# Medians searched with one count to a filter round instead of two, and finished beside the convolutions

## The chip, the core and the metric

The kernel runs on one core of one Trainium2 chip. Its engines work on their own instruction queues and meet at semaphores: TensorE multiplies matrices (PE in the profile), VectorE (DVE), ScalarE (ACT) and GpSimd (POOL) do the rest, and SyncE (SP) issues the DMAs. The metric is the device time of one launch in microseconds.

## The reference, cut to what matters

Two layers run on 16 images of 64 channels of 128x128. The first adds, for each image and channel, the negative part of the channel's median, and filters up and down with a ReLU between; the second gates the spectrum of the image, and lets its pixels attend to 320 keys and values that two strided convolutions make.

```python
q_in = jnp.quantile(x.reshape(B, C, -1), 0.5, axis=-1)
x = x + jax.nn.relu(-q_in)[:, :, None, None]
y = upfirdn2d(x, lpf, up=2, padding=6, gain=4.0)
y = upfirdn2d(jnp.maximum(y, 0.0), lpf, down=2)
spec = jnp.fft.rfft2(y, norm='ortho'); mag = jnp.abs(spec)
gate = sigmoid(w2 @ gelu(w1 @ mag))
xf = y + jnp.fft.irfft2(spec * gate, s=(128, 128), norm='ortho')
# q = xf @ q_w; k, v from conv(xf, stride 8) and conv(xf, stride 16), layer norm, projections
out = proj(softmax(q @ k.T / 4) @ v) + y
```

The median of 16384 numbers is the mean of the 8192nd and the 8193rd.

## The kernel before, in words

The program first takes the median of the first image with nothing beside it (`first_vector`, `first_scalar`, `first_gpsimd`, `first_tensor`), and then loops 16 times over a body that computes one image and, beside it, the median of the next. A channel lies on two partitions (p and p + 64) with 8192 numbers on each, in `xc`.

The median is written as one generator for each engine (`pe_median`, `act_median`, `pool_median`, `dve_median`, lines 188 to 358). A `yield` ends a piece, and the body calls `slot(n)` at fixed places to put the next n pieces into the engine's queue there. The order of work is so written out by hand; an engine that reaches a piece whose semaphore isn't up yet stands still with all that is behind it.

The pieces before are, in this order:
- 8 of the range: VectorE takes the maximum and the minimum of each quarter (line 273); TensorE swaps the halves; VectorE halves the range 26 times (line 290) and makes the first middle (292).
- 78 of the search, 26 steps of 3 counts. In each VectorE counts the numbers up to the middle in one part (line 300) and ScalarE in the other with a sign (line 236). After three pieces TensorE sums the partitions (lines 201 and 202), VectorE adds the six counts and makes the next middle (307, 310, 312), and GpSimd and VectorE keep the lowest upper bound (252, 254, 304). Both engines wait for the middle before they count on. This is called a step's turnover below.
- 8 of the last count: VectorE counts the numbers up to the bound found (line 318), and TensorE sums (208).
- 17 of the next larger number: for each eighth of `xc` VectorE makes a mask (330), GpSimd adds the numbers (261), and VectorE takes the minimum (335).
- a closing chain of small steps between TensorE and VectorE (lines 214 to 224 and 338 to 358), whose last copy writes `sB` and raises `md_end`.

The body of an image goes through these stages:
- The filter, 37 rounds (n) for 32 pairs of channels, in software pipeline: TensorE widens (459), ScalarE copies (1040), TensorE filters across (469), ScalarE applies the ReLU (1046), TensorE narrows (480), VectorE copies (818), TensorE transposes (499), VectorE copies (832), and every other round TensorE narrows the other way (490) and VectorE copies (825). The rest columns go an own way through bank 7. GpSimd adds the rest rows to 16 channels at once (1216). There are 2 slots in a round from n = 2 on, 70 in all.
- The spectrum, 17 rounds with one slot: lines 517 to 535, copies 853 and 857.
- The magnitudes are transposed (546, copies 866), the gate network follows (556, 569, ScalarE's 1085 and 1090), with 9 slots in its middle.
- The inverse, 16 groups (586 to 599, VectorE's 879 and 885), with 16 slots; what is left of the median comes behind it.
- The turn: 16 groups of 4 transposes (618), which VectorE (895) and ScalarE (1109) copy by turns. No slots. The fourth group waits for `md_end`.
- The convolutions: the first with 32 taps (649), the second with 128 in four parts (638), and between them four pieces of the queries (TensorE 630, ScalarE 1117, VectorE 903, GpSimd 1245 and 1247), and VectorE's addition of the bias to `Z` (911).
- A small chain makes keys and values; meanwhile SyncE lays out the queries with 24 DMAs for a unit (`load_unit`, line 382), two units in a row, and then the maxima (1304). The queries lie over `xc`.
- Attention, 32 tiles.

## Time and profile before

| | |
|---|---|
| median of 3 runs | 12,843.6 us (12,840.56 to 12,852.78) |
| the profiled execution | 12,841.47 us, of it a span of 12,840.0 us |
| TensorE, VectorE, ScalarE, GpSimd busy | 84%, 73%, 57%, 20% |
| mean granted TensorE clock | 0.904 |
| first median, alone | from 18.3 us to 260.9 us |
| one image | 784 us, 16 times |

Times in a profile are microseconds from the span's start. A row of groups says line, engine, operation, what is written and read with shapes, how often; then busy us, the mean ns of one, and the us that the engine stood idle before them, with what ended that. In a row of the timeline the first two numbers are the start and the us that it took; a bracket holds the idle time before. Busy time of TensorE is modelled and overlaps between matmuls. The image looked at below is the sixth; it begins at 4210.1 us.

### The profile page before, as it was taken

How to read it: one execution, taken by the hardware profiler on the slowest of the kernel's cores; microseconds unless marked ns; L12 is line 12 of the kernel's file. 1: busy time of each engine (PE TensorE's matmuls, PEld its weight loads, DVE VectorE, ACT ScalarE, POOL GpSimd, SP SyncE). 2: the span in 40 equal slices, each digit the busy share in tenths (PEclk: the TensorE clock that was granted, in tenths of full speed). 3: DMA queues.
4: the chain of work that ended last, by engine and by line, in shares of the span. 5: the costliest groups of instructions: out<-in, count | busy, mean ns of one | idle time of the engine just before them, and what ended most of it. 6: DMA issues, size and time to landing. Idle time of an engine off the chain costs nothing. (4 is left out here: it accounts for less than half of the span.)

```text
span 12840.0 us, 193091 instructions
## 1 busy us (share of the span) xinstructions
PE 10730.5 (84%) x70049; PEld 5483.5 (43%) x70049; DVE 9433.9 (73%) x16044; ACT 7283.6 (57%) x12109; POOL 2610.8 (20%) x4040
## 2 busy tenths in 40 slices
PE   1797888978879798897988889788897887979889
PEld 1543535334353443534435354353534435344353
DVE  7867667776777767768777686767777677776776
ACT  4656455564646646466464565646566464664646
POOL 1211202112131221302212021121211213122130
PEclk9898898988989899898998989889898898989989
DMA  1021120211202022120211202112021221202212
GB/s 45 18 43 42 39 61 18 50 35 43 57 26 55 21 49 52 28 67 7 54 47 34 66 13 46 43 40 60 18 53 31 45 56 27 53 21 49 52 28 66
DMA packets 169035, 532.27 MB, mean 41 GB/s; under 512 B 64008, under 2 KB 86536, under 8 KB 153168
## 3 DMA queue, kind: packets, MB, share of 16 engines
q1 hardware_dynamic: 168016, 519.00, 17.2%
q8 instruction: 601, 9.85, 0.3%
q14 instruction: 418, 3.42, 0.1%
HBM read 230.38 MB, written 67.11 MB: 23 GB/s over the span
## 5 line engine op out<-in xcount | busy, mean ns | idle before, releaser
L949 DVE TENSOR_REDUCE R<-ps 128x2 f32<-128x640 f32 x4096 | 3195.4, 818 | 941.5 <-PE ps L687 930.6
L1157 ACT ACTIVATE R<-ps 128x512 f32<-128x512 f32 x5120 | 2823.2, 594 | 671.5 <-PE ps L708 645.3
L236 ACT ACTIVATE R<-R,st 128x1475 bf16<-128x1475 f32 x1326 | 2022.9, 1526 | 862.5 <-DVE st L312 687.6
L300 DVE TENSOR_SCALAR_CACHE_REDUCE R<-R,st 128x1255 bf16<-128x1255 f32 x1326 | 2012.0, 1517 | 21.3
L687 PE MATMUL ps<-KST,R 96*128 96x320 bf16 x8192 | 1888.4, 314 | 60.7 <-DVE R L949 50.5
L733 PE MATMUL ps<-R 128*32 128x512 f32 x12288 | 1648.8, 609 | 38.0 <-DVE Wk L903 32.9
L708 PE MATMUL ps<-R,KST 104*128 104x512 bf16 x4096 | 1583.7, 389 | 21.4 <-ACT R L1157 20.6
L687 PEld LDWEIGHTS ps<-KST,R 96*128 96x128 bf16 x8192 | 764.8, 100 | 828.6 <-DVE R L949 313.0
L1245 POOL CAST R<-Wk 128x512 bf16<-128x512 f32 x256 | 283.8, 1109 | 2980.4 <-DVE Wk L903 2980.4
L201 PE MATMUL ps<-st,cst 128*128 128x3 f32 x884 | 176.0, 269 | 697.7 <-DVE R L300 464.4
L480 PE MATMUL ps<-R,cst 128*64 128x512 f32 x2048 | 648.5, 715 | 109.0 <-DVE R L818 109.0
L708 PEld LDWEIGHTS ps<-R,KST 104*128 104x128 bf16 x4096 | 397.8, 98 | 724.8 <-ACT R L1157 457.2
L469 PE MATMUL ps<-R,cst 64*128 64x512 f32 x2048 | 627.4, 692 | 12.7 <-ACT R L1046 12.4
L372 POOL TENSOR_TENSOR R<-R,sB 128x1024 f32<-128x1024 f32 x136 | 255.1, 1897 | 1653.2 <-DMA R<-xh_in 1648.2
L1040 ACT ACTIVATE R<-ps 128x532 f32<-128x532 f32 x512 | 308.0, 601 | 494.0 <-PE ps L459 493.8
L1046 ACT ACTIVATE R<-ps 128x1024 f32<-128x1024 f32 x512 | 521.2, 1018 | 89.9 <-PE ps L469 89.0
L201 PEld LDWEIGHTS ps<-st,cst 128*128 128x128 f32 x884 | 156.5, 215 | 877.7 <-DVE R L300 792.9
L261 POOL TENSOR_TENSOR R<-R 128x1024 f32<-128x1024 f32 x136 | 327.6, 2415 | 963.1 <-DVE R L330 963.1
L1099 ACT ACTIVATE Wk<-ps 128x512 f32<-128x512 f32 x256 | 152.9, 597 | 647.2 <-PE ps L589 647.2
L1152 ACT ACTIVATE Wk<-ps 128x512 f32<-128x512 f32 x512 | 305.7, 597 | 368.7 <-PE ps L733 368.7
L1164 ACT ACTIVATE Wk<-ps 128x256 f32<-128x256 f32 x512 | 196.7, 384 | 554.1 <-PE ps L751 554.1
L879 DVE TENSOR_TENSOR Wk<-R 128x520 f32<-128x520 f32 x256 | 298.1, 1170 | 266.0 <-ACT R L1090 215.5
(208 smaller groups left out, 19968.1 us busy)
## 6 DMA issues: line engine op xcount, KB each, us to landing
R<-R SPq DMA_DIRECT2D x3072, 64.0 KB, 2.4
R<-xh_in SPq DMA_DIRECT2D x136, 512.0 KB, 4.5
out_dram<-Z SPq DMA_DIRECT2D x16, 4096.0 KB, 14.3
R<-xa_in SPq DMA_DIRECT2D x36, 1024.0 KB, 11.4
R<-xb_in SPq DMA_DIRECT2D x34, 1024.0 KB, 12.4
R<-sr_in SPq DMA_DIRECT2D x32, 1024.0 KB, 5.4
R<-sr_in SPq DMA_DIRECT2D x16, 2016.0 KB, 9.2
R<-sr_in SPq DMA_DIRECT2D x16, 1056.0 KB
```

What stands on the lines that cost most here:

```text
L201: e.matmul(P0(NP), lhsT=c("pair"), rhs=cnt[:, 0:NP], start=True, stop=False)
L236: e.activation(junka[:, 0:o2 - o1], xc[:, o1:o2], ACT.Sign, bias=mid, scale=-1.0, accum_out=cnt[:, NP + i:NP + i + 1]).then_inc(md_ca, 1)
L261: e.tensor_tensor(t, t, xs, ALU.add).then_inc(md_tb, 1)
L300: e.tensor_scalar(junk[:, 0:o1 - o0], xc[:, o0:o1], mid, None, ALU.is_le, ALU.add, accum_out=cnt[:, i:i + 1]).then_inc(md_cv, 1)
L469: op = e.matmul(ps[:, 2 + j, :].rearrange("p (c h n) -> p c h n", c=2, h=2), lhsT=ut[r, 133 * j:133 * j + 128], rhs=T1[m % 2][r].rearrange ...
L480: op = e.matmul(ps[64 * j:64 * j + 64, 4, :], lhsT=c(f"d{j}"), rhs=Y[m % 2][:, j, :], start=True, stop=True)
L687: op = e.matmul(ps[:, 2 + 2 * bq + r, 0:320], lhsT=q, rhs=KST[0:96, h0 + r, :], start=True, stop=True)
L708: op = e.matmul(ps[:, g2, :], lhsT=KST[:, h, c0:c0 + 128], rhs=QS[u % 3][:, h, 512 * s4:512 * s4 + 512], start=True, stop=True)
L733: op = e.matmul(ps[32 * h:32 * h + 32, 7, :], lhsT=VX[:, 4 * i + h, :], rhs=PB[:, k, src, :], start=i == 0, stop=i == 2)
L949: e.tensor_reduce(MX[(4 * u + s4) % 2][:, blk_, h0:h0 + 2], ps[:, 2 + 2 * bq:4 + 2 * bq, 0:320], axis=AX.X, op=ALU.max).then_inc(mx, 1)
L1046: e.activation(Y[m % 2], ps[:, 2:4, :], ACT.Relu, scale=4.0).then_inc(yr, 1)
L1157: e.activation(PB[:, t % 2, w, :], ps[:, w % 2, :], ACT.Exp).then_inc(ex, 1)
```

## The change

- The range is the largest magnitude: 4 pieces instead of 8, each one maximum of absolute values, and the search starts at 0. The 26 halvings are one multiplication with a row of constants.
- The last count goes. The 16 masks of the next larger number (512 numbers each now, 16 bit, 0 or 2 to the 100th) are multiplied on TensorE with a pair matrix and summed in a bank, and the count is read from the sum. There are 33 pieces for this instead of 8 and 17.
- The two sums of counts on TensorE take 6 and 3 columns.
- The slots: in the filter one in a round and a second in every fourth, 47 in all instead of 70; 17 in the spectrum as before; 18 instead of 9 from the transposes of the magnitudes to the end of the gate network; none in the inverse; 16 in the turn; 16 in the convolutions, 4 behind the first and 4 behind each of three parts of the second. The rest of the median, the closing chain too, comes behind the last part.
- In a filter round ScalarE's piece stands ahead of the ReLU (1046 before) instead of behind it.
- GpSimd's addition of the rest rows is cut in four, one in each of four rounds (the last block: four in a row).
- SyncE waits for the end of the search before it loads the last taps, and for `md_end` before the queries are laid out.

```diff
-            for i in range(8):
-                yield
-            e.wait_ge(md_cv, NP * STEPS + 8)
-            b7.free(e)
-            e.matmul(P0(8), lhsT=c("pair"), rhs=cnt[:, 0:8], start=True, stop=True).then_inc(md_p, 1)
-            b7.ask()
-            for i in range(17):
-                yield
+            for i in range(17):
+                if i < 16:
+                    e.wait_ge(md_ta, i + 1)
+                    b7.free(e)
+                    for q in range(4):
+                        j = q % 2
+                        op = e.matmul(ps[64 * j:64 * j + 64, 7, 336:464], lhsT=pairb[:, :], rhs=MF[i % 2][:, 128 * q:128 * q + 128],
+                                      start=i == 0 and q < 2, stop=i == 15 and q > 1)
+                    op.then_inc(md_fs, 1)
+                yield
+                if i > 0:
+                    yield
+            b7.reader = (md_r, 1)
+            b7.free(e)
+            e.matmul(P0(1), lhsT=c("pair"), rhs=cnt[:, 0:1], start=True, stop=True).then_inc(md_p, 1)
...
         def pool_median(e):
...
-                    e.tensor_tensor(t, t, xs, ALU.add).then_inc(md_tb, 1)
+                    if i > 1:
+                        e.wait_ge(md_mm, i - 1)
+                    e.tensor_tensor(TF[i % 2], MF[i % 2], xc[:, 512 * i:512 * i + 512], ALU.add).then_inc(md_tb, 1)
...
         def dve_median(e, halves):
...
+                e.tensor_reduce(m1[:, k:k + 1], xc[:, 2048 * k:2048 * k + 2048], axis=AX.X, op=ALU.max,
+                                apply_absolute_value=True).then_inc(md_got, 1)
+                yield
...
-            for k in range(STEPS):
-                e.wait_ge(md_got, 2 + k)
-                e.tensor_scalar(hs[:, k + 1:k + 2], hs[:, k:k + 1], 0.5, None, ALU.mult).then_inc(md_got, 1)
...
+            e.tensor_scalar(hs, c("halves"), hi, None, ALU.mult).then_inc(md_v, 1)
...
-                e.tensor_scalar(junk[:, 0:1024], xc[:, 1024 * i:1024 * i + 1024], hi, None, ALU.is_le, ALU.add,
-                                accum_out=cnt[:, i:i + 1]).then_inc(md_cv, 1)
...
+            for i in range(17):
+                if i < 16:
                     if i > 1:
-                        e.wait_ge(md_mm, i - 1)
-                    e.tensor_scalar(t, xs, hi, BIG, ALU.is_le, ALU.mult).then_inc(md_ta, 1)
+                        e.wait_ge(md_tb, i - 1)
+                        e.wait_ge(md_fs, i - 1)
+                    e.tensor_scalar(MF[i % 2], xc[:, 512 * i:512 * i + 512], hi, BIG, ALU.is_le, ALU.mult).then_inc(md_ta, 1)
                 yield
                 if i > 0:
                     e.wait_ge(md_tb, i)
+                    e.tensor_reduce(mm[:, i - 1:i], TF[(i - 1) % 2], axis=AX.X, op=ALU.min).then_inc(md_mm, 1)
                     yield
+            e.wait_ge(md_fs, 16)
+            e.tensor_reduce(cnt[:, 0:1], ps[:, 7, 336:464], axis=AX.X, op=ALU.add).then_inc(md_r, 1)
...
# tensor, vector, scalar and gpsimd, in each filter round
-                slot(1 if n > 1 else 0)
+                slot(1 if n >= P or n % 4 == 0 < n else 0)
# tensor, the inverse, and the turn
-                    slot(1)
-            for _ in med:
-                pass
...
-                    op = e.transpose(ps[:, 4 + k, 128 * i:128 * i + 128], XF[:, 2 * v:2 * v + 2, :].rearrange("p w c -> p (w c)"),
+                    op = e.transpose(ps[:, k, 128 * i:128 * i + 128], XF[:, 2 * v:2 * v + 2, :].rearrange("p w c -> p (w c)"),
                                      c("ident"))
                 op.then_inc(xt_ps, 1)
+                slot(1)
...
             op.then_inc(c1_ps, 1)
+            slot(4)
             for j in range(1, 4):
                 stage(0, j, 6)
                 conv2(j - 1)
+                slot(4)
             conv2(3)
+            for _ in med:
+                pass
...
# gpsimd
+                    for q in range(i, i + 1 if b < 3 else 4):
+                        rows = Z[:, 16 * b + 4 * q:16 * b + 4 * q + 4, :]
+                        e.tensor_tensor(rows, rows, ZS[:, 4 * q:4 * q + 4, :], ALU.add).then_inc(zad, 1)
# sync
+            e.wait_ge(md_v, STEPS + 2)
             e.dma_start(TAP2[:, 65:128, :], sr2w[:, 65:128, :]).then_inc(in_w2[2], 16)
+            e.wait_ge(md_end, 1)
             load_unit(e, 0)
```

The slots move instructions on every engine. In VectorE's queue in the filter stood, in the second half of the rounds before (818, 825 and 832 are a round's copies, 300 a count, 307 to 312 and 304 the turnover):

```order
L307 TENSOR_REDUCE st<-ps 128x1
L310 TENSOR_SCALAR st<-st 128x1
L312 SCALAR_TENSOR_TENSOR st<-st 128x1
L300 TENSOR_SCALAR R,st<-R,st 128x1255
L304 TENSOR_TENSOR st<-st 128x1
L818 COPY R<-ps 128x512
L825 COPY Z<-ps 128x512
L832 COPY R<-ps 128x2x256
L300 TENSOR_SCALAR R,st<-R,st 128x1256 x2
```

and there stands now (811, 818 and 825 are the same copies):

```order
L307 TENSOR_REDUCE st<-ps 128x1
L310 TENSOR_SCALAR st<-st 128x1
L312 SCALAR_TENSOR_TENSOR st<-st 128x1
L300 TENSOR_SCALAR R,st<-R,st 128x1255
L811 COPY R<-ps 128x512
L818 COPY Z<-ps 128x512
L825 COPY R<-ps 128x2x256
L798 COPY R<-ps 96x261
L300 TENSOR_SCALAR R,st<-R,st 128x1256
L304 TENSOR_TENSOR st<-st 128x1
```

Between two sets of copies stood two counts, and there stands one; the small operation 304 has moved behind the second count.

In TensorE's queue the turn and the convolutions were, before (618 transposes, 630 queries, 649 and 638 the convolutions):

```order
L618 MATMUL ps<-cst,R 128x128 x64
L630 MATMUL ps<-R,cst 128x512
L649 MATMUL ps<-R 64x256 x32
L630 MATMUL ps<-R,cst 128x512
L638 MATMUL ps<-R 64x64 x32
```

and the beginning of the turn is now (606 transposes, 203 and 204 the sums of the last search step, 212 the masks' matmuls):

```order
L606 MATMUL ps<-cst,R 128x128 x4
L203 MATMUL ps<-st,cst 128x6
L204 MATMUL ps<-st,cst 128x3
L212 MATMUL ps<-Wk,pairb 64x128 x4
L606 MATMUL ps<-cst,R 128x128 x4
L212 MATMUL ps<-Wk,pairb 64x128 x4
L606 MATMUL ps<-cst,R 128x128 x8
```

and from the turn's last groups into the convolutions (619, 638 and 627 the queries and the convolutions):

```order
L606 MATMUL ps<-cst,R 128x128 x8
L212 MATMUL ps<-Wk,pairb 64x128 x4
L619 MATMUL ps<-R,cst 128x512
L638 MATMUL ps<-R 64x256 x32
L212 MATMUL ps<-Wk,pairb 64x128 x8
L619 MATMUL ps<-R,cst 128x512
L627 MATMUL ps<-R 64x64 x32
```

Every second group of transposes has four matmuls of a mask behind it, which wait for VectorE.

In VectorE's queue the turn was eight copies (895), then queries (903) and bias (911):

```order
L358 COPY sB<-ps 128x64
L895 COPY R<-ps 128x512 x8
L903 SCALAR_TENSOR_TENSOR Wk<-ps,cst,R 128x512
L911 TENSOR_TENSOR Z<-Z,cst 128x64x32
L903 SCALAR_TENSOR_TENSOR Wk<-ps,cst,R 128x512
```

and it is now, from the first copy (885) on (321 a mask, 325 a minimum):

```order
L885 COPY R<-ps 128x512
L307 TENSOR_REDUCE st<-ps 128x1
L314 TENSOR_TENSOR st<-st 128x1
L321 TENSOR_SCALAR Wk<-R,st 128x512 x2
L885 COPY R<-ps 128x512
L325 TENSOR_REDUCE st<-Wk 128x1
L321 TENSOR_SCALAR Wk<-R,st 128x512
```

A minimum and a mask stand behind each copy, and in the convolutions two of each stand behind each piece of the queries and bias.

## Rows read from the trace of the kernel before

**Rows 1.** Busy us by stretch, sixth image, with granted clock and DMA.
```profile
core 0: us, PE busy (x) PEld busy (x) DVE busy (x) ACT busy (x) POOL busy (x), PEclk, DMA share, GB/s
4210.00:4420.00 210.00, 163.10 (x866) 78.29 (x865) 181.83 (x329) 145.06 (x196) 37.69 (x115) 0.85 0.06 13
4482.00:4515.00 33.00, 22.70 (x119) 17.60 (x119) 16.32 (x28) 13.36 (x15) 5.10 (x2) 0.66 0.00 1
4515.00:4570.00 55.00, 50.68 (x553) 35.56 (x554) 46.96 (x56) 9.55 (x16) 14.18 (x6) 0.95 0.24 91
4570.00:4612.00 42.00, 40.90 (x391) 27.27 (x388) 17.97 (x18) 9.10 (x14) 15.11 (x8) 1.00 0.04 12
4612.00:4645.00 33.00, 20.27 (x66) 7.00 (x66) 21.19 (x35) 3.46 (x8) 18.81 (x30) 0.56 0.53 93
```

**Rows 2.** Timeline of ScalarE, filter rounds of the sixth image: start us, us.
```profile
4249.11 0.59 ACT L1040 ACTIVATE R<-ps 128x532 f32<-128x532 f32 x1
...
4392.56 0.61 ACT L1040 ACTIVATE R<-ps 128x532 f32<-128x532 f32 x1 [0.19 <-PE ps L459]
```

**Rows 3.** Groups by line, of the page.
```profile
L236 ACT ACTIVATE R<-R,st 128x1475 bf16<-128x1475 f32 x1326 | 2022.9, 1526 | 862.5 <-DVE st L312 687.6
L300 DVE TENSOR_SCALAR_CACHE_REDUCE R<-R,st 128x1255 bf16<-128x1255 f32 x1326 | 2012.0, 1517 | 21.3
```

**Rows 4.** Groups by line and shape, whole span.
```profile
L818 DVE COPY R<-ps 128x512 f32<-128x512 f32 x512 | 351.3, 686 | 72.6 <-PE ps L480 71.9
L273 DVE TENSOR_REDUCE st<-R 128x1 f32<-128x2048 f32 x136 | 305.2, 2277 | 8.9 <-DMA R<-xa_in 7.8 <-DMA R<-xb_in 1.1
L895 DVE COPY R<-ps 128x512 f32<-128x512 f32 x128 | 88.6, 692 | 27.8 <-PE ps L618 27.8
```

**Rows 5.** Timeline of ScalarE in the first median, which nothing else runs beside.
```profile
51.98 1.53 ACT L236 ACTIVATE R<-R,st 128x1475 bf16<-128x1475 f32 x1 [1.82 <-DVE st L312]
...
58.72 1.53 ACT L236 ACTIVATE R<-R,st 128x1475 bf16<-128x1475 f32 x1 [1.82 <-DVE st L312]
```

**Rows 6.** Timeline of VectorE in the spectrum, sixth image.
```profile
4445.28 0.69 DVE L853 COPY Wk<-ps 128x512 f32<-128x512 f32 x1
...
4447.76 0.69 DVE L853 COPY Wk<-ps 128x512 f32<-128x512 f32 x1
...
4451.33 0.69 DVE L853 COPY Wk<-ps 128x512 f32<-128x512 f32 x1
```

**Rows 7.** Timeline of VectorE, start of the search, sixth image.
```profile
4240.84 4.87 DVE L290 TENSOR_SCALAR st<-st 128x1 f32<-128x1 f32 x26
```

**Rows 8.** Timeline of the end of the first median, nothing beside it.
```profile
220.73 1.28 DVE L318 TENSOR_SCALAR_CACHE_REDUCE R<-R,st 128x1024 bf16<-128x1024 f32 x1
...
232.24 1.41 DVE L330 TENSOR_SCALAR R<-R,st 128x1024 f32<-128x1024 f32 x2
...
239.85 1.80 DVE L330 TENSOR_SCALAR R<-R,st 128x1024 f32<-128x1024 f32 x1
241.58 1.21 DVE L335 TENSOR_REDUCE st<-R 128x1 f32<-128x1024 f32 x1
241.74 2.34 POOL L261 TENSOR_TENSOR R<-R 128x1024 f32<-128x1024 f32 x1 [0.63 <-DVE R L330]
...
257.47 0.37 PE L214 MATMUL ps<-cst,st 128*1 128x128 f32 x1 [25.54 <-DVE st L338]
...
260.69 0.23 DVE L358 COPY sB<-ps 128x64 f32<-128x64 f32 x1 [0.78 <-PE ps L224]
```

**Rows 9.** Timeline of VectorE beside the addition of line 1216.
```profile
4422.29 3.09 DVE L304 TENSOR_TENSOR st<-st 128x1 f32<-128x1 f32 x1
```

**Rows 10.** Timeline of VectorE in the convolutions, sixth image.
```profile
4595.34 0.75 DVE L903 SCALAR_TENSOR_TENSOR Wk<-ps,cst,R 128x512 f32<-128x512 f32 x1 [12.96 <-ACT R L1117]
...
4600.05 0.75 DVE L903 SCALAR_TENSOR_TENSOR Wk<-ps,cst,R 128x512 f32<-128x512 f32 x1 [1.76 <-ACT R L1117]
```

**Rows 11.** Timeline of SyncE's queue at the start of attention, sixth image.
```profile
4609.51 30.59 SPq L382 DMA_DIRECT2D R<-R  x48
```

More of the change, by code:

```diff
@@ L188, in pe_median @@
         def pe_median(e, b7):
-            for _ in range(8):
+            for _ in range(4):
                 yield
@@ L192, in pe_median @@
             b7.free(e)
-            e.matmul(P0(2), lhsT=c("swap"), rhs=pm, start=True, stop=True).then_inc(md_p, 1)
+            e.matmul(P0(1), lhsT=c("swap"), rhs=pm[:, 0:1], start=True, stop=True).then_inc(md_p, 1)
             b7.ask()
             for k in range(STEPS):
-                for i in range(NP):
+                for _ in range(NP):
                     yield
@@ L226, in act_median @@
         def act_median(e):
-            for _ in range(8):
+            for _ in range(4):
                 yield
@@ L246, in pool_median @@
                 mid = mids[:, k % 2:k % 2 + 1]
-                for i in range(NP):
+                for _ in range(NP):
                     yield
@@ L548, in tensor @@
                 op.then_inc(mt_ps, 1)
+                slot(1 if grp % 3 else 0)
             for grp in range(9):
@@ L559, in tensor @@
                     op.then_inc(h_ps, 1)
-                slot(1)
+                slot(1 if grp % 3 else 0)
             for grp in range(9):
@@ L573, in tensor @@
                 op.then_inc(g_ps, 1)
+                slot(1 if grp % 3 else 0)
             for n in range(18):
@@ L839, in vector @@
                     e.tensor_copy(VM, ps[0:80, 7, 0:128]).then_inc(mq, 1)
-                slot(1 if n > 1 else 0)
+                slot(1 if n >= P or n % 4 == 0 < n else 0)
             for i in range(2):
@@ L866, in vector @@
                 e.tensor_copy(MAGT[:, 512 * grp:512 * grp + 128 * np_], ps[:, 5 + grp % 2, 0:128 * np_]).then_inc(mgt, 1)
-            for grp in range(9):
+                slot(1 if grp % 3 else 0)
+            for grp in range(12):
                 slot(1)
@@ L911, in vector @@
                 e.tensor_tensor(zj, zj, c("pb").unsqueeze(2).to_broadcast([128, C, 32]), ALU.add).then_inc(zb, 1)
+                slot(4)
+            for _ in med:
+                pass
             e.wait_ge(xt_ps, 16)
@@ L1040, in scalar @@
                     e.activation(T1[n % 2].rearrange("p h c n -> p h (c n)"), ps[:, 0:2, 0:266], ACT.Copy).then_inc(t1, 1)
+                slot(1 if n > 1 else 0)
                 m = n - 1
@@ L1046, in scalar @@
                     e.activation(Y[m % 2], ps[:, 2:4, :], ACT.Relu, scale=4.0).then_inc(yr, 1)
-                slot(1 if n > 1 else 0)
                 if n >= 8 and n % 8 == 0:
@@ L1085, in scalar @@
                     e.activation(HID[0:rows, o:o + w], ps[0:rows, k, 0:w], ACT.Gelu).then_inc(gelu, 1)
-                slot(1)
+                slot(1 if grp % 3 else 0)
             for grp in range(9):
@@ L1091, in scalar @@
                              ps[:, 2 + grp % 2, 0:128 * np_].rearrange("p (k c) -> p k c", c=C), ACT.Sigmoid).then_inc(sig, 1)
+                slot(1 if grp % 3 else 0)
             for n in range(18):
@@ L1229, in gpsimd @@
                                     ALU.add).then_inc(mag, 1)
-            for grp in range(9):
-                slot(1)
-            for n in range(18):
-                if n >= 2:
-                    slot(1)
-            for _ in med:
-                pass
+            slot(18)
+            slot(16)
             def stage(g, j, bk):
@@ L1250, in gpsimd @@
                 stage(0, j, 6)
+                slot(4)
+            for _ in med:
+                pass
             steps = 0
```

127 lines of the change are left out of this document (48 added, 79 removed).

## The prediction, made before the changed kernel was run

> **What bounds the kernel now.** I first cut one image into its stages by the busy time of each stretch, then looked for what fills a filter round, then for what a search step costs alone. An image takes 784 us, and some 435 of them come before attention's first scores; the change touches only these. In the filter's 210 us VectorE is busy for 182, ScalarE 145, TensorE 163 at a granted clock of 0.85; in the gate network's 33 us all are half idle; in the inverse's 55 us TensorE is busy for 50.7, in the turn and the convolutions' 42 us for 40.9; then come 33 us in which a chain makes keys and values [rows 1]. From the 7th to the 31st round, 24 of them, the filter takes 143.45 us, or 5.98 a round [rows 2]. Its two slots hold two counts of 1.52 us on VectorE and 1.53 on ScalarE [rows 3], and a round's copies are 0.69 each, two and a half of them [rows 4]: 3.04 + 1.7 = 4.8 us of VectorE. The missing 1.2 us are turnovers, two in three rounds. Alone, a step of three counts takes 6.74 us [rows 5], so a turnover costs 6.74 - 3 x 1.65 = 1.8 us on ScalarE (1.65 us is a count with the reading of its sum, by the 1.53 and the start of the next behind it). Where one slot stands in a round, in the spectrum, rounds follow after 2.48 us, and after 3.57 where a turnover falls between [rows 6]: 1.1 us. So in the filter the median is on the path, counts and turnovers both, and taking some away shortens it. Everywhere else it was hidden well or nearly.
>
> **The first median, once.** Its second half waits for data until 28 us, so of the four reductions less only two count: -4.5 us, by 2.277 [rows 4]. The 26 halvings, 4.87 us, become one operation: -4.8 [rows 7]. From the last count's start to the first mask are 11.5 us, which go, and one sum more comes, 0.9. The masks took 232.24 to 257.47, 25.2 us for 8 [rows 8]: a mask waits for GpSimd, then a mask (0.7), and an addition (2.34) follow each other. 16 halves do the same in 16 x (0.4 + 1.2) = 25.6. Together -19.5 us.
>
> **The filter, each image.** Four reductions less: -9.1; the halvings -4.8. The 25 rounds from there on keep 31 of 50 counts and 10.3 of 16.7 turnovers. VectorE: 1.25 x 1.57 + 1.8 for copies = 3.8; turnovers, one in 2.4 rounds, at 1.1 to 1.8, are 0.45 to 0.75; so 4.2 to 4.5. TensorE is busy for 163 / 37 = 4.4 us a round now, at the clock of 0.85 [rows 1], and has to do all of it but a third of the sums. It is so near that neither hides behind the other; I take 4.6, with 4.2 and 5.1 for ends. 25 x (5.98 - 4.6) = -34.5. The last 5 rounds keep their slots. A small operation of VectorE stood 3.09 us behind GpSimd's addition of the rest rows as the spectrum began [rows 9]; of a quarter it could be held a quarter as long: -2. Sum -50 (-60 to -38).
>
> **The spectrum** keeps its 17 slots: 0.
>
> **The gate network.** 18 slots, 6 steps, where 9 were. In the transposes VectorE has 6 x 1.57 + 9 copies (5.8) + two turnovers (1.6) = 17 us. Behind them ScalarE is later: 12 counts of 1.65, of which the last is beside the inverse, 18.1; its own 13.4 [rows 1]; of four turnovers two in full and one in part, 4.4: 36. 53 us against 33: +20 (+16 to +25). This is where counts no longer have a cover.
>
> **The inverse.** TensorE is busy for 50.7 of 55 us; that is what can be won: up to -4.3, taken as -3.5 since VectorE has no masks left there and the closing chain is gone.
>
> **The turn.** Eight copies of VectorE with the idle time before them are (88.6 + 27.8) / 16 = 7.3 us an image [rows 4]. TensorE's queue now holds a mask's matmuls behind every second group. A ring closes: group of transposes (0.45 at full clock, double at half), VectorE's copy 0.69, a minimum (0.6, half of 1.21), a mask (0.4), the matmuls (0.3), handoffs 0.2: 2.6 to 3.1 for two groups, where 0.9 was. Of the last, most is at half clock, for TensorE is idle over half of it, as in the stretch behind the convolutions (0.56 granted, 20.3 of 33 us busy [rows 1]). 7 such, and the search's last turnover with two masks at the start, 4: 23 to 26 us. +17.
>
> **The convolutions.** Four parts with 32 more matmuls. The queries follow each other after 4.71 us [rows 10]; VectorE now has query 0.75, bias 2.3, two minima and two masks, 2.0, behind 0.8 of handoff: 5.9, and TensorE stands before the second mask. Two such rounds cost +1.5 to +3.6 each, the third has one mask to wait for, +1.5; the first convolution starts at half clock, +1.5. +8.
>
> A mask behind GpSimd's work is the open point. Alone, masks of 0.7 us took 1.80 while an addition ran [rows 8]. The Trainium skill (SBUF — State Buffer, Who interferes with whom) says that a tensor_scalar in a two-port mode and a GpSimd instruction block each other for a whole instruction, and a reduction never does. By that rule, and this trace agrees with 1.80 against 0.7, a mask also waits for GpSimd's subtraction of the queries and for the addition of the mask before.
>
> **The closing chain** took 3.45 us, 257.47 to 260.92 [rows 8], and has one sum more, 4.3. It stood in the inverse's end; now keys and values wait for it, and SyncE's queue, which began 2.5 us before the convolutions' end (4609.51 against 4612.0 [rows 1, 11]), begins 4.4 behind it. 24 copies of 0.64 us and a landing come before the first maxima, so +4.3 to +6.9: I take +5.4.
>
> **Sum.** -50 + 20 - 3.5 + 17 + 8 + 5.4 = -3.1 us an image, 16 times -50; with -19.5 the profiled 12,841.5 become 12,772. The median of the runs is 2.1 us more than the profiled execution; I say 12,775 us. Two large terms stand against each other: rounds that get 1.4 us shorter, and places where the same counts and masks have less cover.
>
> **Rivals.**
> - Rounds of 4.2 us. For it: VectorE's sum allows it. Against: TensorE's 4.4. It gives 25 x 0.4 x 16 = 160 less: 12,615.
> - Masks never blocked. The convolutions then cost 3.5 and not 8, the turn 15: 6.5 x 16 = 104 less, 12,670. The page's rule speaks against it; with the rule in force at every mask of the convolutions they cost 10.5: +40, 12,815, at the edge of what can be told from before.
> - Slower: TensorE stands in its own queue before masks, and works at half clock when it goes on. The turn then takes 4 us for two groups, and the first convolution, 15 us at the full clock of 1.00 that [rows 1] show, has half of it at 1.2 GHz. That is +7 and +7.5, 14.5 an image, +232: 13,005. For it: 0.56 of the clock where TensorE is busy 20 of 33 us. Against: the ring's parts add up to 3.1 at most. It decides from where turn and convolutions take over 72 us together (they are 42 now, 67 in my sum).
> - Filter rounds of 5.1: TensorE's busy 4.4 is the bound and the waits of the coupled engines come on top. +12.5 an image, +200: 12,975, slower.
> - The change takes out the counts it says; 25 rounds with 31 counts stand in the code. Only the gain could be missing, which is the rival before.
>
> **How the numbers follow.** My forecast has 0.40, and its own range is 12,700 to 12,830 us; rounds of 4.2 us 0.12; masks never blocked 0.07, blocked everywhere 0.07; the slower rival 0.20; rounds of 5.1 us 0.14. Under 0.2%, some 26 us, a measurement of this kernel can't tell from no change. Faster: 0.38 of the forecast, 0.12, 0.07, 0.01: 0.58. The same: 0.02, and most of blocked everywhere, 0.05, and 0.03 of the two slower cases: 0.10. Slower: 0.32. The range leaves out the outer parts of the first and third rivals: 12,590 to 12,990.
>
> **What would show it.** Right: the filter from first widening to the spectrum in 155 to 172 us, rounds of 4.3 to 5.0; the gate network 49 to 58 us; the turn 20 to 28 us with TensorE waiting for masks; the convolutions with 4.7 stretched to 6 to 8; `md_end` about 4 us behind the last convolution, and keys and values behind it. The masks, 512 numbers, would take 0.4 us free and over 1 us behind GpSimd. Wrong: rounds over 5 us; a gate network under 45 us, which would say that counts hide beside sigmoids; a turn under 15 us; an attention that changes its length.

## The result, and the profile after

The changed kernel takes 12,803.8 us (median, 12,786.4 to 12,843.3), the kernel before in the same session 12,850.9 (12,834.3 to 12,871.4), 20 runs each. The ratio is 0.9967, 95% interval 0.9960 to 0.9974: faster by a third of a per cent. The profiled execution took 12,798.9 us (span 12,797.6), 42.6 less than that of before. I had said 12,775.

A small sum of large terms, as forecast. The medians over the 16 images, in us from an image's first matmul, cut at the first matmul of each stage (the last line is the mean from one image's start to the next, and the line above it what is left of that):

| stage | before | after | change | predicted |
|---|---|---|---|---|
| first median, once | 280.0 | 259.9 | -20.1 | -19.5 |
| filter, with the search's range | 210.0 | 168.8 | -41.2 | -50 |
| spectrum | 62.6 | 56.5 | -6.1 | 0 |
| gate network | 33.3 | 51.2 | +17.9 | +20 |
| inverse | 53.9 | 49.8 | -4.1 | -3.5 |
| turn | 9.0 | 28.1 | +19.1 | +17 |
| convolutions | 33.1 | 39.7 | +6.6 | +8 |
| last convolution to first scores | 33.5 | 39.1 | +5.6 | +5.4 |
| first scores to the next image | 349.5 | 350.5 | +1.0 | 0 |
| an image | 784.9 | 783.7 | -1.2 | -3.1 |

16 times -1.2 and -20.1 are -39; the spans differ by 42.4.

The sixth image by stretch, in the order of the table without the spectrum (turn and convolutions, one row in [rows 1], are two here; columns: us, busy us and instructions of each engine, granted clock, DMA share, GB/s):

```profile
4177.70:4346.20 168.50, 141.41 (x841) 68.81 (x841) 135.04 (x237) 115.90 (x160) 39.80 (x116) 0.94 0.06 13
4402.70:4454.00 51.30, 33.45 (x141) 24.80 (x141) 36.80 (x71) 39.10 (x50) 2.48 (x12) 0.50 0.00 0
4454.00:4504.00 50.00, 49.76 (x544) 35.26 (x544) 24.15 (x32) 10.24 (x18) 0.00 (x0) 0.94 0.18 65
4504.00:4532.00 28.00, 18.21 (x105) 13.87 (x106) 14.47 (x28) 4.78 (x8) 10.51 (x11) 0.63 0.20 74
4532.00:4572.00 40.00, 34.77 (x336) 20.17 (x337) 20.68 (x24) 4.30 (x6) 25.18 (x16) 0.96 0.01 2
4572.00:4611.00 39.00, 24.24 (x93) 9.11 (x89) 23.24 (x48) 3.46 (x8) 17.82 (x27) 0.55 0.50 82
```

The filter's clock rose from 0.85 to 0.94, the gate network's fell to 0.50, where TensorE is busy for 33 of 51 us and waits in between; the inverse is full. The turn, nearly full before, has TensorE busy for 18 of 28 us at 0.63. ScalarE's copy of the widened rows in rounds 7 and 31 of this filter (counted from 0), as in [rows 2]:

```profile
4204.59 0.61 ACT L1034 ACTIVATE R<-ps 128x532 f32<-128x532 f32 x1
4318.35 0.61 ACT L1034 ACTIVATE R<-ps 128x532 f32<-128x532 f32 x1 [0.65 <-PE ps L453]
```

That is 113.76 / 24 = 4.74 us a round, where it was 5.98. Now the turn, two groups of the ring on VectorE, GpSimd and TensorE (timeline: start us, us, engine, line, idle before and its releaser):

```profile
4510.70 0.69 DVE L885 COPY R<-ps 128x512 f32<-128x512 f32 x1 [2.57 <-PE ps L606]
4511.31 0.67 DVE L325 TENSOR_REDUCE st<-Wk 128x1 f32<-128x512 f32 x1
4511.90 0.48 DVE L321 TENSOR_SCALAR Wk<-R,st 128x512 bf16<-128x512 f32 x1
4512.44 0.30 PE L212 MATMUL ps<-Wk,pairb 128*64 128x128 bf16 x4 [1.08 <-DVE Wk L321]
4512.46 1.17 POOL L270 TENSOR_TENSOR Wk<-Wk,R 128x512 f32<-128x512 bf16 x1 [2.19 <-DVE Wk L321]
4512.67 1.09 PE L606 MATMUL ps<-cst,R 128*128 128x128 f32 x8
4513.37 0.69 DVE L885 COPY R<-ps 128x512 f32<-128x512 f32 x1 [0.98 <-PE ps L606]
...
4515.10 0.42 PE L212 MATMUL ps<-Wk,pairb 128*64 128x128 bf16 x4 [1.33 <-DVE Wk L321]
...
4515.45 1.97 PE L606 MATMUL ps<-cst,R 128*128 128x128 f32 x8
4516.60 0.69 DVE L885 COPY R<-ps 128x512 f32<-128x512 f32 x1 [1.56 <-PE ps L606]
```

VectorE waits for TensorE's group (L606), TensorE for VectorE's mask (L321): neither is full. A turn of this ring of waits takes 2.67 us with 8 matmuls at full clock (1.09) and 3.23 at half (1.97). In the convolutions the queries on VectorE, 4.71 us apart in [rows 10], follow each other after 7.40, with two minima (L325) and two masks (L321) between:

```profile
4550.67 0.75 DVE L894 SCALAR_TENSOR_TENSOR Wk<-ps,cst,R 128x512 f32<-128x512 f32 x1 [10.91 <-ACT R L1108]
4551.34 2.28 DVE L902 TENSOR_TENSOR Z<-Z,cst 128x2048 f32<-128x2048 f32 x1
4553.54 0.68 DVE L325 TENSOR_REDUCE st<-Wk 128x1 f32<-128x512 f32 x1
4554.14 0.47 DVE L321 TENSOR_SCALAR Wk<-R,st 128x512 bf16<-128x512 f32 x1
4554.53 0.68 DVE L325 TENSOR_REDUCE st<-Wk 128x1 f32<-128x512 f32 x1
4555.12 0.78 DVE L321 TENSOR_SCALAR Wk<-R,st 128x512 bf16<-128x512 f32 x1
4558.07 0.75 DVE L894 SCALAR_TENSOR_TENSOR Wk<-ps,cst,R 128x512 f32<-128x512 f32 x1 [2.17 <-ACT R L1108]
```

The second mask stands beside GpSimd's subtraction of the query, which ends at 4555.62, and takes 0.78 us where the first took 0.47. Over the whole trace 48 of the 112 masks in the convolutions took 0.8 us, and none of the 144 in the turn.

The median ends 3.9 us behind the last convolution (4573.3), and keys and values begin behind it:

```profile
4577.00 0.22 DVE L352 COPY sB<-ps 128x64 f32<-128x64 f32 x1 [0.78 <-PE ps L234]
4577.25 0.41 DVE L907 MEMSET R<- 64x424 f32 x1
```

### The profile page after: what moved, and what is told of

It is laid out like the page before. It is cut to its first block and busy times, and to the rows that moved or that the text cites. A ratio compares the mean times of both kernels' runs of the same rounds, so it can differ in the third digit from the quotient of the medians.

```text
span 12797.6 us, 195926 instructions
## 1 busy us (share of the span) xinstructions
PE 10782.9 (84%) x71137; PEld 5569.1 (44%) x71137; DVE 8883.3 (69%) x15501; ACT 7238.6 (57%) x12109; POOL 2641.9 (21%) x4368
## 5 line engine op out<-in xcount | busy, mean ns | idle before, releaser
L300 DVE TENSOR_SCALAR_CACHE_REDUCE R<-R,st 128x1255 bf16<-128x1255 f32 x1326 | 2011.3, 1517 | 20.8
L463 PE MATMUL ps<-R,cst 64*128 64x512 f32 x2048 | 569.2, 630 | 102.8 <-ACT R L1041 94.9
L203 PE MATMUL ps<-st,cst 128*128 128x6 f32 x884 | 187.1, 283 | 540.3 <-DVE R L300 217.4
L366 POOL TENSOR_TENSOR R<-R,sB 128x1024 f32<-128x1024 f32 x136 | 254.9, 1895 | 1642.4 <-DMA R<-xh_in 1636.8
L474 PE MATMUL ps<-R,cst 128*64 128x512 f32 x2048 | 562.8, 628 | 21.1 <-ACT R L1041 21.1
L1108 ACT ACTIVATE R<-ps,cst 128x512 bf16<-128x512 f32 x256 | 175.9, 687 | 670.7 <-PE ps L619 670.7
L1041 ACT ACTIVATE R<-ps 128x1024 f32<-128x1024 f32 x512 | 517.6, 1011 | 44.5 <-PE ps L463 44.5
L1143 ACT ACTIVATE Wk<-ps 128x512 f32<-128x512 f32 x512 | 305.7, 597 | 369.2 <-PE ps L726 369.2
L878 DVE TENSOR_TENSOR R<-ps,Z 128x512 f32<-128x512 f32 x256 | 269.7, 1063 | 350.8 <-PE ps L595 350.8
L262 POOL TENSOR_SCALAR st<-st 128x1 f32<-128x1 f32 x442 | 99.5, 225 | 1974.6 <-DVE st L307 1961.1
```

Source lines behind the costliest of these rows:

```text
L203: e.matmul(P0(2 * NP), lhsT=c("pair"), rhs=cnt[:, 0:2 * NP], start=True, stop=False)
L300: e.tensor_scalar(junk[:, 0:o1 - o0], xc[:, o0:o1], mid, None, ALU.is_le, ALU.add, accum_out=cnt[:, i:i + 1]).then_inc(md_cv, 1)
L463: op = e.matmul(ps[:, 2 + j, :].rearrange("p (c h n) -> p c h n", c=2, h=2), lhsT=ut[r, 133 * j:133 * j + 128], rhs=T1[m % 2][r].rearrange ...
L474: op = e.matmul(ps[64 * j:64 * j + 64, 4, :], lhsT=c(f"d{j}"), rhs=Y[m % 2][:, j, :], start=True, stop=True)
L1041: e.activation(Y[m % 2], ps[:, 2:4, :], ACT.Relu, scale=4.0).then_inc(yr, 1)
```

## The experiments

Each kernel ran 4 to 11 times, by turns with the kernel before; the ratio is to that one. "Changed" is 12,804 us, from its own session.

| run | us | ratio, 95% interval | against changed |
|---|---|---|---|
| addition in one piece | 13,096 | 1.0196 (1.0182 to 1.0210) | +292 |
| search in the inverse | 12,628 | 0.9825 (0.9811 to 0.9838) | -176 |
| mask matmuls one mask later | 12,583 | 0.9792 (0.9779 to 0.9805) | -221 |
| masks in the inverse | 12,492 | 0.9724 (0.9711 to 0.9737) | -312 |
| before, with the range alone | 12,634 | 0.9836 (0.9823 to 0.9849) | -170 |
| counts back in the filter | 12,824 | 0.9985 (0.9976 to 0.9993) | +20 |
| closing chain in the next chain | 12,738 | 0.9918 (0.9906 to 0.9931) | -66 |
| three moves | 12,290 | 0.9564 (0.9552 to 0.9576) | -514 |
| before, range and two edits | 12,592 | 0.9802 (0.9789 to 0.9816) | -212 |
| raise behind the first count | 12,790 | 0.9955 (0.9941 to 0.9969) | -14 |
| ScalarE's piece behind the ReLU | 12,716 | 0.9889 (0.9873 to 0.9905) | -88 |
| four moves | 12,202 | 0.9500 (0.9487 to 0.9513) | -602 |

**The addition in one piece.**

```diff
-                if n >= 12 and n % 8 > 3:
-                    b, i = n // 8 - 1, n % 8 - 4
+                if n >= 12 and n % 8 == 4:
+                    b = n // 8 - 1
...
-                    for q in range(i, i + 1 if b < 3 else 4):
-                        rows = Z[:, 16 * b + 4 * q:16 * b + 4 * q + 4, :]
-                        e.tensor_tensor(rows, rows, ZS[:, 4 * q:4 * q + 4, :], ALU.add).then_inc(zad, 1)
+                    rows = Z[:, 16 * b:16 * b + 16, :]
+                    e.tensor_tensor(rows, rows, ZS, ALU.add).then_inc(zad, 1)
```

> The changed kernel with GpSimd's addition of the rest rows in one piece again, as before the change; all else is the changed kernel, which took 12,804 us. Theory A: the four pieces are what made the spectrum 6.1 us an image shorter (62.6 to 56.5) though its slots are the same, and part of what the filter gained. Then the spectrum is back at 60 to 63 us, a small operation of VectorE stands about 3 us behind the last addition again, and the kernel takes 12,870 to 12,930 us. Theory B: the pieces are worth only that one stall, 2 us an image as the prediction had it, and the spectrum stays near 57 us: 12,825 to 12,845 us.

Both theories were far too low: 18 us an image. The filter took 184.1 us instead of 168.8, its rounds 5.26 instead of 4.74; the spectrum 58.7, not 60 to 63. In that kernel's sixth image, one of the four additions:

```profile
4375.10 4.54 POOL L1207 TENSOR_TENSOR Z<-Z,R 128x2048 f32<-128x2048 f32 x1
...
4376.19 0.08 DVE L300 DVE_READ_ACCUMULATOR R<-R,st 128x1 f32 x1
4376.19 3.48 DVE L304 TENSOR_TENSOR st<-st 128x1 f32<-128x1 f32 x1
...
4379.59 1.51 DVE L300 TENSOR_SCALAR_CACHE_REDUCE R<-R,st 128x1256 bf16<-128x1256 f32 x1
```

An operation on one number a partition, begun 1.1 us into the addition, ended with it. VectorE loses 3.3 us, and count, copies and turnover stand behind it in its queue. The groups of the two small operations with two inputs in that kernel, and then in the changed one (busy, mean ns):

```profile
L312 DVE SCALAR_TENSOR_TENSOR st<-st 128x1 f32<-128x1 f32 x425 | 199.6, 470 | 14.9
L304 DVE TENSOR_TENSOR st<-st 128x1 f32<-128x1 f32 x425 | 172.0, 405 | 0.0
```

```profile
L312 DVE SCALAR_TENSOR_TENSOR st<-st 128x1 f32<-128x1 f32 x425 | 124.4, 293 | 14.9
L304 DVE TENSOR_TENSOR st<-st 128x1 f32<-128x1 f32 x425 | 70.8, 166 | 0.0
```

The two are shorter by (199.6 - 124.4) + (172.0 - 70.8) = 176 us, 11 an image. If all of that is on the path, it is 11 of the 18; the other 7 are not shown. (In this run TensorE and SyncE also wait for the whole addition and no longer for a quarter of it, and that was not run apart.) The Trainium skill (SBUF — State Buffer, Who interferes with whom) says that a VectorE instruction with two SBUF inputs contends with a GpSimd instruction that reads SBUF; by that rule both small operations are held and the counts are not. The trace agrees: the 3.48 us are of an operation with two such inputs, and the counts (L300), with one, have a mean of 1,517 ns in both kernels.

The kernel before had such stalls too, and the page of lines says so:

```profile
L312 DVE SCALAR_TENSOR_TENSOR st<-st 128x1 f32<-128x1 f32 x425 | 198.4, 467 | 14.9
L304 DVE TENSOR_TENSOR st<-st 128x1 f32<-128x1 f32 x425 | 112.8, 265 | 0.0
```

Of these, 32 of L312 and 16 of L304 took over 1.5 us, three an image, and not only the one of [rows 9].

**Search in the inverse.** Of the gate network's 18 slots two stay; the same on each engine, here TensorE's:

```diff
                 op.then_inc(mt_ps, 1)
-                slot(1 if grp % 3 else 0)
+                slot(1 if grp in (1, 2) else 0)
...
                     e.matmul(ps[:, 2 + k, :], lhsT=c("edft"), rhs=RR[k], start=True, stop=True).then_inc(xi_ps, 1)
+                    slot(1)
```

> The changed kernel with 16 of the gate network's 18 slots moved into the inverse, where the kernel before had 16. Theory A: counts cost about 1 us a slot in the gate network (+17.9 us for 18) and 0.26 in the inverse (53.9 against 49.8 for 16), since TensorE fills the inverse and VectorE and ScalarE have gaps there. Then the gate network takes 34 to 37 us, the inverse 53 to 56, and the kernel 12,804 less 16 x 12 to 14: 12,580 to 12,615 us. Theory B: what the gate network loses is the same everywhere, since a step's turnover hangs on three engines; then the inverse takes 62 us or more and the kernel 12,720 to 12,800 us.

Theory A in its kind; its sizes were off, and the kernel at 12,628 us is 13 above its range. The gate network took 29.4 us (254.9 - 225.5), below the range, the inverse 58.7 (313.6 - 254.9), 8.9 more and not 4: 0.56 us a slot against 1.4 in the gate network. The 0.26 came from the inverse of before, whose slots held masks and minima and no count at all.

**TensorE's matmuls over a mask one mask later.**

```diff
                 b7.ask()
+            yield
+            yield
             for i in range(17):
                 if i < 16:
                     e.wait_ge(md_ta, i + 1)
```

> The changed kernel with TensorE's matmuls over a mask issued two slots, that is one mask, later, so that in the turn and in the convolutions TensorE no longer stands before a mask that VectorE has yet to make. Theory A: the turn is a ring, TensorE's group, VectorE's copy, minimum and mask, and TensorE's matmuls over it. Without the last link the turn falls from 28.1 to what VectorE needs, 17 to 21 us, the convolutions from 39.7 to 36 to 38, and the kernel takes 12,640 to 12,690 us. Theory B: VectorE's own line (copy, minimum behind GpSimd's addition, mask) sets the pace, whatever TensorE does; the turn stays at 25 to 28 us, the kernel at 12,770 to 12,810 us.

Theory A, with more gain than it said: the turn takes 15.2 us (28.1), below VectorE's 17 to 21, since copy, minimum and mask start 0.60, 0.59 and 0.40 us after one another, 1.59 a turn of the ring. The convolutions took 38.1, and the kernel 57 us less than the range's lower end. In its turn TensorE waits 0.26 us for a mask instead of over 1, and does its groups at full clock:

```profile
4442.75 0.68 DVE L887 COPY R<-ps 128x512 f32<-128x512 f32 x1
4442.88 0.30 PE L214 MATMUL ps<-Wk,pairb 128*64 128x128 bf16 x4 [0.26 <-DVE Wk L323]
4443.11 1.09 PE L608 MATMUL ps<-cst,R 128*128 128x128 f32 x8
4443.35 0.67 DVE L327 TENSOR_REDUCE st<-Wk 128x1 f32<-128x512 f32 x1
4443.94 0.47 DVE L323 TENSOR_SCALAR Wk<-R,st 128x512 bf16<-128x512 f32 x1
4444.34 0.67 DVE L887 COPY R<-ps 128x512 f32<-128x512 f32 x1
```

(These lines have other numbers: the copy is L887, the minimum L327, the mask L323.) VectorE waits for nothing: the mask whose matmuls stand behind a group in TensorE's queue now stands ahead of that group's copy in VectorE's, and no longer behind it. It is 1.59 us from copy to copy, where it was 2.67 to 3.23, and the granted clock of the turn is 1.00 in every image, where it was 0.54 to 0.61. So most of the turn's price was the place of these matmuls in TensorE's queue: two empty slots pay back 13 of its 19 us, the lower clock that came with the waits included.

**Masks in the inverse**, two slots behind each of its groups, none in the turn and the convolutions, the mask's buffers in R5:

```diff
                     e.matmul(ps[:, 2 + k, :], lhsT=c("edft"), rhs=RR[k], start=True, stop=True).then_inc(xi_ps, 1)
+                    slot(2)
+            for _ in med:
+                pass
...
                 op.then_inc(xt_ps, 1)
-                slot(1)
...
             op.then_inc(c1_ps, 1)
-            slot(4)
```

> The changed kernel with its 32 slots of masks and minima in the inverse, two behind each group, and none in the turn and in the convolutions; the closing chain stands ahead of the turn, as before the change (the mask's buffers lie in the counts' junk for that). Theory A: the inverse has the gaps. The turn is back at 9 to 10 us (-18), the convolutions at 33 (-6.5), keys and values 5.6 us earlier, against it the inverse's 49.8 become 57 to 60, and the closing chain ahead of the turn costs 3 to 4: -18 to -22 us an image, 12,450 to 12,520 us. Theory B: the ring of mask, GpSimd's addition, minimum and TensorE's matmuls takes 3 us or more a mask wherever it stands, with a group of the inverse on top: the inverse takes 75 us or more, and the kernel 12,700 to 12,810 us.

Theory A. Inverse 59.4 us (336.1 - 276.7, closing chain and all), turn 11.2, convolutions 33.0, keys and values as before. Masks and closing chain cost 9.6 us there and 2.2 in the turn, 11.8 in all, against 19.1 + 6.6 + 5.6 = 31.3 in their three places: the period is 19.5 us shorter.

**Before, with the range alone.** The kernel before, with two parts of the change (four reductions, one product with the constants), and four slots fewer in the filter:

```diff
-                for i in range(2):
-                    op = e.tensor_reduce(m1[i][:, k:k + 1], xc[:, 2048 * k:2048 * k + 2048], axis=AX.X,
-                                         op=(ALU.max, ALU.min)[i])
...
+                e.tensor_reduce(m1[0][:, k:k + 1], xc[:, 2048 * k:2048 * k + 2048], axis=AX.X, op=ALU.max,
+                                apply_absolute_value=True).then_inc(md_got, 1)
...
-                slot(1 if n > 1 else 0)
+                slot(1 if n > 5 else 0)
```

> The kernel before with one part of the change alone: the bracket from the largest magnitude (four reductions instead of eight, the steps' sizes by one product with a row of constants), and four slots fewer in the filter, so that all later pieces stand where they stood. Two counts a round, the last count and the masks are those of before. Theory A: what the changed kernel gained at the filter's start, 11.2 us an image, and 9 in the first median is this part's and needs none of the rest: 12,851 less 16 x 11 to 14 and 9: 12,620 to 12,670 us, faster than the changed kernel. Theory B: the halvings and reductions lay partly beside TensorE's first rounds, and the gain there comes from the slots that follow; then 12,720 to 12,780 us.

Theory A. The filter took 197.2 us (210.0), the first median 9.7 us less, and no other stage up to the first scores moved by more than 0.3. This one part is worth 1.64%, more than the whole change: all the rest together takes 170 us of it back.

**Counts back in the filter.**

```diff
-                slot(1 if n >= P or n % 4 == 0 < n else 0)
+                slot(1 if n > 6 else 0)
...
-                slot(1 if grp % 3 else 0)
+                slot(0)
```

> The changed kernel with the 18 slots of the gate network put back into the filter: 65 slots there instead of 47 (a second slot in each round from the 7th on, as before), spectrum 17, gate network none. Theory A: the filter loses what it had gained by giving slots away, (210.0 - 168.8 - 11.2 of the range) / 19 counts = 1.6 us a count, so 18 cost 28 us; the gate network gives back 17.9 and is at 33: +10 us an image, 12,950 to 12,990 us. Theory B: rounds of the filter with two counts are no longer as long as before, since turnovers are cheaper with the raise behind the second count and the addition in pieces: the filter loses under 20 us, and the kernel takes 12,780 to 12,840 us.

Neither. The time, 12,824 us, lies in theory B's range, but not by its reason: the filter lost not under 20 us but 29.0, as theory A had it (197.8), and the gate network without any slot took 23.9 and not 33, and gave back 27.3. A count costs 1.6 us in the filter and 1.5 in the gate network: moving 18 of them from one to the other hardly changes the time (+20 us, 0.2%).

**The closing chain between the steps of keys and values**, and the loads of queries freed earlier. Its steps get slots of their own:

```diff
             conv2(3)
-            for _ in med:
-                pass
+            slot(2)
             e.wait_ge(kd, 2)
...
             e.matmul(ps[0:64, 2, 0:320], lhsT=c("pair")[:, 0:64], rhs=XP, start=True, stop=True).then_inc(kp, 1)
+            slot(1)
...
-            e.wait_ge(md_end, 1)
+            e.wait_ge(md_tb, 16)
             load_unit(e, 0)
```

> The changed kernel with the median's closing chain laid between the steps of the chain that makes keys and values, and with SyncE's first loads of queries waiting for the last use of the picture's buffer and no longer for the median's end. Theory A: both chains are waits on one another engine, and fit into each other: the stretch from the last convolution to the first scores falls from 39.1 to 33 to 36 us, 12,710 to 12,760 us. Theory B: first scores hang on SyncE's loads or on VectorE's small operations, whose number stays; 12,780 to 12,810 us.

Theory A: 33.6 us (429.7 - 396.1), as before the change.

**Three moves together.**

> The changed kernel with three moves together: 16 search slots from the gate network into the inverse (alone -176 us), TensorE's mask matmuls one mask later (alone -221 us), and the closing chain between the steps of keys and values. If the three are independent places on the path, the gains add: 12,804 - 176 - 221 - 60 = 12,350 us, 12,320 to 12,400. If the search's end at the inverse's last groups delays the turn's first masks, or the mask matmuls meet the chain, 10 us an image or more are lost of it: 12,450 to 12,520 us, no better than the masks in the inverse.

The moves are independent enough, and the time is 30 us under the range and 51 better than the measured single gains make it (12,804 - 176 - 221 - 66 = 12,341). A part can be placed: with only the search moved, turn and convolutions took 70.0 us, 2.2 more than in the changed kernel (67.8); with the three moves they took 53.8, only 0.5 more than with the later matmuls alone (53.3). That is 1.7 us an image, 27 of the 51. Why the search's move made them longer, and the rest, stay open.

**Before, with the range and two more edits** (the addition in pieces and the raise behind the second count, as in the change):

> The kernel before with the magnitude range (alone 12,634 us), and with two small edits of the change beside it: GpSimd's addition of the rest rows in four pieces, and the raise of the upper bound behind the second count of a step instead of the first. Theory A: small operations of VectorE that stand behind the whole addition cost this kernel too, 3 to 4.5 us each, two or three an image, and the spectrum's late start (13.4 us to its first square, 7.5 in the changed kernel) is the same thing: the start falls to 7 or 8 us, the filter by 3 to 8 us: 12,634 less 130 to 220: 12,410 to 12,500 us. Theory B: the pieces were worth 18 us an image only because rounds of 4.7 us have no slack; in rounds of 6 us they are hidden, and the spectrum's start hangs on where the search's step falls (62 counts ahead of it, two over a full step; 43 in the changed kernel, one over): 12,590 to 12,640 us.

The time is theory B's: 42 us, 2.6 an image, where the pieces are worth 18 in the changed kernel. But less was taken away, too. The two small operations were busy for 198.1 + 112.9 us with the range alone, and for 167.1 + 79.4 here: 64.5 us less, 4.0 an image, against 11. So a good part of the difference is that less stalling went away. What is left, 2.6 out of 4.0 here and 18 out of 11 there, is in line with theory B's slack in long rounds, which was not run apart. Of the spectrum, the first square falls from 13.4 us behind its first matmul to 11.1, not to 7.5.

**The raise behind the first count.**

```diff
-                    if i == 1 and k:
+                    if i == 0 and k:
```

> The changed kernel with the raise of the upper bound behind the first count of a step again, as before the change; all else is the changed kernel (12,804 us). It needs GpSimd's two small operations on the bound, which start when a step's sum is there. Theory A: behind the first count it stands 1.5 us earlier, in the time in which GpSimd has just begun an addition that holds a small operation of VectorE up: the spectrum's start is later by 1 to 6 us and the filter by 0 to 3: 12,820 to 12,900 us. Theory B: with the additions in pieces it is held 1.3 us at most, a few times an image: 12,800 to 12,820 us.

Theory B, with the time 10 us under its range; the 14 us below the changed kernel are 0.1%, not to be told from nothing. The spectrum's start stayed at 7.4.

**ScalarE's piece behind the ReLU.**

```diff
-                slot(1 if n > 1 else 0)
                 m = n - 1
                 if 0 <= m < P:
...
                     e.activation(Y[m % 2], ps[:, 2:4, :], ACT.Relu, scale=4.0).then_inc(yr, 1)
+                slot(1 if n > 1 else 0)
```

> The changed kernel with ScalarE's first piece of a filter round behind the ReLU again, as before the change, and not ahead of it. Theory A: ahead of the ReLU the count fills the time in which ScalarE would wait for TensorE's product; behind it, each round is longer by a part of that wait, 0.2 to 0.4 us: 12,880 to 12,960 us. Theory B: ScalarE has 1 us or more to spare in a round of 4.7 us, and its order sets nothing: 12,790 to 12,820 us. Theory C: ahead of the ReLU the count delays TensorE's next product, and the old order is the faster one: 12,700 to 12,780 us.

Theory C. TensorE's two groups that need the ReLU (L1041), in the changed kernel and then in this one (busy, mean ns, idle before):

```profile
L463 PE MATMUL ps<-R,cst 64*128 64x512 f32 x2048 | 569.2, 630 | 102.8 <-ACT R L1041 94.9 <-issue 6.7
L474 PE MATMUL ps<-R,cst 128*64 128x512 f32 x2048 | 562.8, 628 | 21.1 <-ACT R L1041 21.1
```

```profile
L474 PE MATMUL ps<-R,cst 128*64 128x512 f32 x2048 | 559.7, 625 | 38.8 <-DVE R L811 38.8
L463 PE MATMUL ps<-R,cst 64*128 64x512 f32 x2048 | 555.1, 619 | 5.1 <-issue 5.1
```

TensorE stood 116 us for the ReLU, held back by a count of 1.5 us, and stands for it no longer; 124 us of idle time became 44, and a round takes 4.52 us. (The four runs lie between 12,687 and 12,732 us, so the 88 are good to some 20.)

**Four moves.**

> The three moves together (search slots in the inverse, mask matmuls one mask later, closing chain between the steps of keys and values: 12,290 us) with the fourth that the runs point to: ScalarE's first piece of a filter round behind the ReLU again (alone -88 us). Theory A: the filter is a stage apart from the other three, so the gains add: 12,290 - 88 = 12,200 us, 12,180 to 12,225. Theory B: with another end of the filter the search enters the spectrum and the inverse differently, and half of it is lost: 12,240 to 12,290 us.

Theory A: 12,202 us, 5.0% under the kernel before. Its sixth image by stretch, stages as above:

```profile
3985.30:4148.80 163.50, 140.03 (x841) 68.41 (x841) 134.17 (x237) 118.01 (x160) 39.72 (x116) 0.93 0.06 13
4207.50:4235.50 28.00, 22.25 (x123) 17.44 (x123) 9.84 (x19) 15.95 (x18) 0.41 (x2) 0.62 0.00 1
4235.50:4294.40 58.90, 51.58 (x564) 37.66 (x565) 50.12 (x83) 33.74 (x48) 2.06 (x10) 0.96 0.15 55
4294.40:4310.40 16.00, 14.85 (x102) 10.96 (x102) 13.56 (x26) 4.78 (x8) 9.90 (x11) 0.79 0.34 130
4310.40:4348.40 38.00, 34.21 (x360) 21.61 (x359) 22.35 (x27) 4.30 (x6) 25.72 (x16) 0.97 0.02 3
4348.40:4382.90 34.50, 22.49 (x73) 8.37 (x74) 22.78 (x46) 3.46 (x8) 18.89 (x30) 0.55 0.56 91
```

In the inverse TensorE and VectorE are both nearly full, which is what the cover of a stage looks like when it is used.

## Why the prediction came out as it did

The forecast stood: faster, by two sets of large terms against each other. That the total came out within 29 us is in part luck. The filter gained 8.8 us an image less than I said, 141 us in all, and the spectrum, put at nothing, gained 6.1, 98 us in all. Term by term:

- **The first median**: -19.5 against -20.1. Right.
- **The filter's start**: said -13.9, measured -11.2 (38.6 to 27.4 us at the copy of round 7); the range alone gave 12.8. The term was a quarter too large.
- **The filter's rounds**: said 4.6, measured 4.74. Right in size, and in part by luck: it priced "VectorE 4.2 to 4.5, TensorE 4.4" as two loads, and two edits that are in neither load move the figure, from 4.52 to 4.74 and to 5.26. The addition in pieces, which I priced at -2 us an image for one stall, is worth 18: without it rounds take 5.26 us and the change makes the kernel 2% slower. That is the term that was mis-sized most; I read the one held operation of [rows 9] at the filter's end and did not ask where the other three additions fall, though the kernel before had three long stalls an image. And ScalarE's piece ahead of the ReLU, which the prediction gave no price at all, costs 88 us, 5.5 an image. The two errors have opposite signs.
- **The spectrum**: said 0, measured -6.1. The slots are the same; the first square comes 6.0 us earlier, and why stays open. In the kernel before, the pieces with the raise bring 2.3 of it; in the changed kernel the raise brings none, and the addition in one piece doesn't delay it either (7.1 us). For the rest there are correlations only: kernels that enter the spectrum with 62 counts done (before, range alone, range and edits) start at 11.1 to 13.4 us, those with 43 or 61 done (a step's turnover one slot later) at 6.5 to 7.5. The end of GpSimd's last addition parts the same kernels as well: 5.4 to 5.8 us behind the spectrum's first matmul in the three late ones, 1.2 behind it or earlier in the others. No run changed either alone.
- **The gate network**: said +20, measured +17.9, and the range of 49 to 58 us held (51.2). Without slots it takes 23.9, so the nine of before cost 9.4 us and the eighteen 27.3. The two can't be compared slot by slot: the nine were seven pieces of the last count and two masks, without ScalarE and without turnovers, the eighteen are counts of the search on both engines with six turnovers. The size was right; the single loads it was added from were not run apart.
- **The inverse**: -3.5 against -4.1. Right, but read only for what the slots there had cost, not for what they could hold.
- **The turn**: +17 against +19.1, with the ring as described, at 2.67 and 3.23 us against 2.6 to 3.1. The run with the later matmuls shows that the place of the mask's matmuls in TensorE's queue is the cause of 13 of the 19; the other 6 stay, in a turn in which VectorE is busy for 13.3 of 15.2 us. The slower rival had this mechanism too, at 4 us a turn of the ring; turn and convolutions took 67.8 us together, not over 72.
- **The convolutions**: +8 against +6.6. A mask took 0.47 or, beside GpSimd's subtraction, 0.78 us; "over 1 us" was too much. It is held only while the subtraction still runs, here for 0.5 us.
- **The closing chain**: +5.4 against +5.6. Right; all of it could be hidden.

Of the rivals, rounds of 4.2 and of 5.1 us are out at 4.74. "Masks never blocked" would have given a turn of 24 us and convolutions of 36.6; it is out by both times, though its premise was true in the turn, where no mask was held, and the turn was long all the same. "Blocked everywhere" is out as well: 48 masks of 112. What the prediction lacked is not in the list: that one of its edits was worth five times the whole (1.64% against 0.33%). Its own terms held this, -13.9 an image and -9.3 once for the range, 232 us together, and 211 were measured; it never set them against the rest.

## What to carry to other kernels

Take such a change apart before it is judged as one: here -0.3% was -1.6% from one part and +1.3% from the others. Where work is laid beside other work, read of each stage which engine is full and put it where all that it needs have room; and since an engine works through its queue in order, put the instruction that needs another engine's result one step behind the place where that result is due. Two empty slots were worth 221 us.

## What the runs showed of the hardware

- A VectorE operation on one number a partition with two inputs in SBUF took 3.48 us beside a GpSimd addition of 4.54 us, where the median of all 425 is 0.16. How often it happens hangs on where the addition falls: over the kernel the two small operations were busy for 372 us with whole additions in the changed kernel, 311 in the kernel before, 195 with additions in quarters. The same edit was worth 18 us an image in the changed kernel, with rounds of 4.7 us, and 2.6, another edit with it, in the kernel before with the range alone, with rounds of 6.
- The turn's transposes took 1.09 us for eight at full clock and 1.97 at half. In the changed kernel both come, with TensorE idle for over 1 us in each 2.7 to 3.2 us of the ring (0.63 granted in the stretch); with 0.26 us idle in 1.6, in the run with the later matmuls, the stretch has 1.00 granted and all full groups took 1.07 to 1.10. The mean granted clock of the whole was 0.892 changed, 0.907 with the later matmuls and 0.923 with four moves. It doesn't rise with every removed wait: with ScalarE's piece behind the ReLU, where 80 us of TensorE's idle time went, it was 0.890 to 0.894.
